# Two-layer decoder on one core: remainders of exponentials on two engines, a fourth staging buffer, scores by row groups

## The reference

```python
# layer 0
x = ln(einsum('bes,st->bet', x, Wr + Wc) + bias ...)        # mixing by decay matrices
s = einsum('bhqd,bhkd->bhqk', q, k) / 4                     # 16 heads of 16, 64 keys
attn = softmax(where(causal, s, min)); x = ln(x + (attn @ v) @ Wout.T)
e = argmax(x @ router_w); score = sigmoid(max(x @ router_w)) # 8 experts, one for each token
x = ln(x + expert_e(x * score) + shared(x))
# layer 1
x = ln(x + spectral_attention(x))      # DFT of normalised q, k; running sums over tokens
x = ln(x + latent_attention(x, ctx))   # 16 heads over 64 latent keys, softmax with causal mask
w = ternary(w_gate_up), ternary(w_proj)  # bf16, groups of 64: q = clip(round(w/mean|w|), -1, 1)
x = ln(x + swiglu(x, w) * rms)
```

## Time and profile before

| | us |
|---|---|
| median of 3 runs | 615.67 (613.36 to 617.16) |
| the profiled execution | 610.82 |
| its span, first to last instruction | 609.5 |
| PE busy | 553.6 |
| DVE busy | 472.8 |
| POOL busy | 389.4 |
| ACT busy | 369.8 |

### The profile page before, as it was taken

One profiled execution on the slowest core, in us unless ns is written; L12 is line 12 of the kernel. 1 busy time (PEld: TensorE's weight loads), 2 busy tenths in 40 slices (PEclk: granted clock), 3 DMA queues, 4 the chain that ended last, 5 costly groups with the idle time before them and its releaser, 6 DMA issues. The chain is left out here.

```text
span 609.5 us, 14270 instructions
## 1 busy us (share of the span) xinstructions
PE 553.6 (91%) x5331; PEld 436.6 (72%) x5331; DVE 472.8 (78%) x1266; ACT 369.8 (61%) x783; POOL 389.4 (64%) x467
## 2 busy tenths in 40 slices
PE   5789999889777999977899999999999999999995
PEld 3657887768654766643477888887877778889994
DVE  6896978796889675568899586689888898867656
ACT  5767588667643644545376567647665666655663
POOL 5839657678770440079999938775686644343896
PEclk9998999999899999999899999999999999999999
DMA  9132223104657443472010000022001200000001
GB/s 351 46 140 91 69 74 121 40 24 140 194 173 225 128 146 104 160 170 37 0 31 3 2 1 2 2 54 53 2 20 34 52 3 1 2 1 3 1 2 69
DMA packets 23696, 42.19 MB, mean 69 GB/s; under 512 B 3834, under 2 KB 18300, under 8 KB 23612
## 3 DMA queue, kind: packets, MB, share of 16 engines
q1 hardware_dynamic: 19900, 35.56, 17.9%
q0 software_dynamic: 3072, 4.20, 3.4%
q10 hardware_dynamic: 656, 1.52, 0.8%
HBM read 31.96 MB, written 10.35 MB: 69 GB/s over the span
## 5 line engine op out<-in xcount | busy, mean ns | idle before, releaser
L1761 DVE TENSOR_TENSOR first<-bank,first 128x512 f16<-128x512 f32 (+2 forms) x127 | 69.7, 564 | 14.0 <-ACT first L1627 5.9
L2216 POOL TENSOR_TENSOR first<-first 128x512 f16<-128x512 f32 x44 | 52.5, 1197 | 22.4 <-ACT first L1648 19.7
L1070 PE MATMUL bank<-wide,first 128*128 128x256 f16 (+4 forms) x199 | 54.3, 283 | 8.7 <-DVE first L1761 3.2
L1077 PE MATMUL bank<-c_first,first 128*128 128x128 f32 (+1 forms) x318 | 51.4, 280 | 3.8 <-ACT first L1580 1.8
L1071 PE MATMUL bank<-wide,first 128*128 128x256 f16 (+4 forms) x199 | 54.1, 282 | 0.0
L1072 PE MATMUL bank<-wide,first 128*128 128x256 f16 (+4 forms) x199 | 53.1, 281 | 0.0
L1077 PEld LDWEIGHTS bank<-c_first,first 128*128 128x128 f32 (+1 forms) x318 | 36.3, 140 | 12.2 <-ACT first L1580 4.7
L2194 POOL TENSOR_TENSOR first<-first,minus_half 128x2 f32<-128x2 f32 x30 | 22.3, 744 | 26.9 <-DVE first L1860 26.8
L2239 POOL DMA_INDIRECT wide<-made_rows,made_at x8 | 13.0, 1621 | 38.9 <-DMA made_rows<-first 35.0
L1761 DVE TENSOR_TENSOR wide<-bank,wide 128x512 f16<-128x512 f32 (+1 forms) x52 | 33.1, 651 | 4.8 <-ACT wide L1593 2.4
L2314 POOL TENSOR_TENSOR wide<-wide 128x512 f16<-128x512 f32 x16 | 18.6, 1160 | 23.4 <-ACT wide L1737 23.4
(11 more groups left out here) (465 smaller groups left out, 2108.4 us busy)
## 6 DMA issues: line engine op xcount, KB each, us to landing
wide<-in_fold SPq DMA_DIRECT2D x8, 992.0 KB, 5.2
wide<-in_expert SPq DMA_DIRECT2D x8, 768.0 KB, 4.7
wide<-in_ternary SPq DMA_DIRECT2D x8, 384.0 KB, 4.1
first<-sent_rows SPq DMA_DIRECT2D x20, 128.0 KB, 2.2
made_rows<-first SPq DMA_DIRECT2D x20, 128.0 KB, 1.9
x_mid<-first SPq DMA_DIRECT2D x7, 256.0 KB, 2.7
first<-in_x SPq DMA_DIRECT2D x4, 256.0 KB, 3.0
wide<-x_mid SPq DMA_DIRECT2D x4, 256.0 KB, 3.0
```

Of the source, the lines that this page charges most:

```text
L1070: mm(o, lhs[0], rhs[0], start=start, stop=False)
L1077: last = nc.tensor.transpose(view[0:m, c0:c0 + n], src, kc["identity" if dt == F32 else "identity_bf"][0:n, 0:n])
L1761: return V.tensor_tensor(lo, whole, hi, ALU.subtract)
L2216: G.tensor_tensor(B.pl[r], B.pf, B.ph[r], ALU.subtract).then_inc(says("ex_l"), 1)
```

## The change

Parts of it:

- Remainders of the first layer's exponentials: g = 0 and 2 stay on POOL (`ex_l`), g = 1 and 3 go to DVE (`ex_v`). The remainders of the gate and up weights of experts 4 and 6 go from POOL to DVE (`eg_lv`).
- A fourth staging buffer of 1560 words for three ternary blocks, laid over the shared expert's gate and up weights (`w_sgu`, not `w_sd`), so that its first load waits for all `rt` and `sh` of the first layer. Buffers 0 and 1 then have no ternary blocks. `t1` and `t2` move, and a lane of the second layer in `wide` ends earlier (`LANE1`).
- Maxima in four row groups: `mx` is now 128x(2x128) bf16, the 4 heads of group n at columns 32n to 32n + 3; `mt` is two 128x128 transposes in bf16, `mt_c` copies 128 rows, and in the first layer `minus_head` multiplies on the 32 rows of the group, with the bank as the inner loop. The causal matmuls come last. The second layer's `sc` keeps its matmuls on 128 rows.
- The count of a unit (`cnt`) is f32, `rk_seen` of unit 7 is gone, and `tb` sums `seen[7]` and the two `hot` tiles of unit 7 in three matmuls. `tb_cnt` has 3 waited steps for 5, `tb_tile` 5 for 9.
- Plan: new lengths, a part `begun` of 72 units ahead of the first loads, `keep_warm` from unit 2500 on, and another `RANKS`, so another order on every engine.

```diff
-    h = np.arange(NH)[:, None, None, None]
-    sel = -(h == 2 * np.arange(NP)[None, :, None, None] + np.arange(2)[None, None, :, None]).astype(np.float32)
-    c["minus_head"] = bf(np.concatenate([np.broadcast_to(sel, (NH, NP, 2, L)).reshape(NH, NP, P), np.zeros((P - NH, NP, P))]))
+    row = np.arange(P)[:, None, None, None]
+    pair, own = np.arange(NP)[None, :, None, None], np.arange(2)[None, None, :, None]
+    sel = -(row == P // ROWS * (pair // 2) + pair % 2 * 2 + own).astype(np.float32)
+    c["minus_head"] = bf(np.broadcast_to(sel, (P, NP, 2, L)).reshape(P, NP, P))
...
-EARLY_FOLDS, THIRD = 4, 5
+EARLY_FOLDS, THIRD, FOURTH = 4, 5, 3
...
-       + [("d", 0), ("b", 0)] + [("h", n) for n in range(EARLY_FOLDS, NPREP)] + [("f", n) for n in TERNARY[THIRD:]])
-TURNS = [[turn for n, turn in enumerate(ROW) if n % 2 == b] for b in range(2)] + [[("f", n) for n in TERNARY[:THIRD]]]
+       + [("d", 0), ("b", 0)] + [("h", n) for n in range(EARLY_FOLDS, NPREP)] + [("f", n) for n in TERNARY[THIRD + FOURTH:]])
+TURNS = [[turn for n, turn in enumerate(ROW) if n % 2 == b] for b in range(2)] + [[("f", n) for n in TERNARY[:THIRD]], [("f", n) for n in TERNARY[THIRD:THIRD + FOURTH]]]
...
+ON_VECTOR = (4, 6)
+
+
+def gate_up_rest(e):
+
+    return "eg_lv" if e in ON_VECTOR else "eg_lo"
+
+
+def shares_rest(u, g):
+
+    return "ex_v" if u < NB and g % 2 else "ex_l"
...
-    p.keep_warm(80, 0.7, 900)
+    p.keep_warm(80, 0.7, 2500)
...
+    LATE_STAGE = STAGES - 4 * (C * D + FSTAGE)
+    stages = [wide.tile([STAGE if n < 2 else FSTAGE]) for n in range(3)]
+    k.t1 = wide.tile([2, HEADS * DC], F32, 96)
+    k.t2 = wide.tile([HEADS, DC])
+    stages.append(wide.back(LATE_STAGE).tile([FSTAGE]))
     k.W = []
-    for n in range(3):
+    for n, stage in enumerate(stages):
...
-        B.mT = (a if n < LANES else shared).tile([S], BF16)
+        B.mx = (a if n < LANES else shared).tile([T, P], BF16)
...
-        B.cnt = a.tile([NE], F16)
+        B.cnt = a.tile([NE])
...
+        if b == 3 and n == 0:
+            sp.wait_ge(says("rt"), NB)
+            sp.wait_ge(says("sh"), 2 * NB)
...
-        flip(bank("mt", u), [(t * P, NH, lane(u).mx[:, t, :]) for t in range(T)]).then_inc(says("mt"), 1)
+        flip(bank("mt", u)[:, :].bitcast(BF16), [(t * P, P, lane(u).mx[:, t, :]) for t in range(T)], BF16).then_inc(says("mt"), 1)
...
-            for n, b in enumerate(banks):
-                mm(b[:, :].rearrange("p (n s) -> p n s", n=2)[:, :, 0:L], kc["identity_bf"], kc["causal_cols"], start=False, stop=False)
-                for m in range(C):
-                    last = mm(b[:, m * S:(m + 1) * S], kc["minus_head"][:, 2 * n + m, :], B.mT, start=False, stop=(m == C - 1))
+            for m in range(C):
+                for n, b in enumerate(banks):
+                    rows = slice(n * PAIR, (n + 1) * PAIR)
+                    mm(b[:, m * S:(m + 1) * S], kc["minus_head"][rows, 2 * n + m, :], B.mT[rows, :], start=False, stop=False)
+            for b in banks:
+                last = mm(b[:, :].rearrange("p (n s) -> p n s", n=2)[:, :, 0:L], kc["identity_bf"], kc["causal_cols"], start=False, stop=True)
...
-        pe.wait_ge(*done("ex_l", u, g))
+        pe.wait_ge(*done(shares_rest(u, g), u, g))
...
-        pe.wait_ge(*done("rk_seen", NB - 1))
-        mm(bank("tb", 0)[:, 0:NE], kc["all_ones"], k.seen[NB], start=True, stop=True).then_inc(says("tb"), 1)
+        pe.wait_ge(*done("rt_hot", NB - 1))
+        pe.wait_ge(*done("rk_seen", NB - 2))
+        counted = [k.seen[NB - 1]] + [lane(NB - 1).hot[:, t, :] for t in range(T)]
+        b = bank("tb", 0)
+        for n, some in enumerate(counted):
+            last = mm(b[:, 0:NE], kc["all_ones"], some, start=(n == 0), stop=(n == T))
+        last.then_inc(says("tb"), 1)
...
-        fn(lane(u).mT[0:NH, :], bank("mt", u)[0:NH, 0:S], ACT.Copy).then_inc(says("mt_c"), 1)
+        fn(lane(u).mT, bank("mt", u)[:, :].bitcast(BF16)[:, 0:S], ACT.Copy).then_inc(says("mt_c"), 1)
...
+    def eg_lv(u, e):
+        dve.wait_ge(*done("eg_hi", 0, e))
+        rest(k.w_egu[1][:, e, :], k.W[staged("e", e)[0]].eg.rearrange("p c n -> p (c n)"), k.w_egu[0][:, e, :]).then_inc(says("eg_lv"), 1)
...
+        m = lane(u).mx.rearrange("p t (q h) -> p t q h", q=ROWS)
+        return m[:, :, g, 0:4] if u < NB else m[:, g // 2, g % 2 * 2:g % 2 * 2 + 2, 0:4]
...
+    def ex_v(u, g):
+        B, r = lane(u), g % 2
+        dve.wait_ge(*done("ex_h", u, g))
+        dve.wait_ge(*done("ex_f", u, g))
+        if g > 1:
+            dve.wait_ge(*done("pv", u, g - 2))
+        rest(B.pl[r], B.pf, B.ph[r]).then_inc(says("ex_v"), 1)
...
-        dve.step(V.tensor_tensor(tab.cnt, bank("tb", 0)[:, 0:NE], kc["region_base"][:, 0, :], ALU.subtract))
-        dve.step(V.memset(tab.ones8, 1.0))
-        dve.step(V.tensor_scalar(tab.cnt_i, tab.cnt, float(P - 1), None, ALU.add))
+        base, given = kc["region_base"][:, 0, :], bank("tb", 0)[:, 0:NE]
+        V.memset(tab.ones8, 1.0)
+        dve.step(V.scalar_tensor_tensor(tab.cnt_i, given, float(P - 1), base, ALU.add, ALU.subtract))
+        V.tensor_tensor(tab.cnt, given, base, ALU.subtract)
...
+        before, no = slice(0, NE - 1), kc["tile_no"]
+        V.tensor_scalar(tab.past, tab.ends, no, None, ALU.is_le)
+        dve.step(V.scalar_tensor_tensor(tab.tmp, tab.ends, no, tab.nt, ALU.is_le, ALU.mult))
+        V.tensor_reduce(tab.ex, tab.past[:, before], AX.X, ALU.add)
+        V.tensor_scalar(tab.mine, tab.past[:, NE - 1:NE], float(P), float(-P), ALU.mult, ALU.add)
+        dve.step(V.tensor_reduce(tab.first, tab.tmp[:, before], AX.X, ALU.add))
+        V.tensor_copy(k.tile_exp, tab.ex)
+        V.scalar_tensor_tensor(tab.pick8, kc["expert_no"], tab.ex, tab.cnt, ALU.is_equal, ALU.mult)
+        dve.step(V.tensor_scalar(tab.begin1, tab.first, no, -1.0, ALU.subtract, ALU.add))
+        V.tensor_reduce(tab.cap, tab.pick8, AX.X, ALU.add)
+        dve.step(V.tensor_tensor(tab.at, tab.begin1, tab.mine, ALU.mult))
+        dve.step(V.tensor_tensor(tab.at2, tab.at, tab.cap, ALU.min))
+        V.scalar_tensor_tensor(k.tile_rows, tab.ex, float(REGION), tab.at2, ALU.mult, ALU.add).then_inc(says("tb_tile"), 1)
```

179 lines of the change are left out of this document (83 added, 96 removed).

## The result

| | before | after |
|---|---|---|
| median of 8 runs, us | 615.2 (613.4 to 617.2) | 611.2 (609.2 to 612.0) |
| ratio, 95% interval | | 0.9929 [0.9908, 0.9950] |
| profiled execution, us | 610.8 | 609.15 |
| span, us | 609.5 | 607.8 |

What follows compares the result with a forecast made beforehand. No one engine was taken to bound everything: PE the steady part and experts, POOL the filling, DVE fullest in the first layer. Terms -2 - 4 - 0 - 7 + 1 and -2 gave -14: 601.7 us from 615.67, range 588 to 616.

Steps and rivals of the forecast that it cites:

- the filling is not POOL's to give: Second layer's filling: gather, norm and prefix sums bound it, the fourth buffer gives only 2 us; 606.7 to 610.7, chance 0.20.
- Part 4: Second layer's filling, 280 to 320 us: a fourth staging buffer moves ternary blocks earlier; -7 us, between -2 and -14.
- So three are done near 235: Experts' stage: three ternary blocks chained through the new buffer from 180 on, 17 us for one block.
- the change doesn't move the blocks: Staging of ternary blocks: their loads would still be issued after 258; held hardly possible, no chance of its own given.
- POOL's 97%: Filling, 280 to 320 us: POOL busy 38.9 of 40 us, cited as evidence that POOL bounds this stage.
- would hold up an expert: SP's queue: a late ternary block delays the expert loads behind it; 0 to 3 us, taken as 0.
- Part 3: Table of expert rows: table and send start earlier, with fewer waited steps; -4 us, between -1 and -5.
- Part 2: First layer: remainders shared between POOL and DVE; the stage changes by -2 us, from -8 to +16.
- the 16 us of the rival: First layer: DVE, filled as before at 84%, bounds it and the stage takes 16 us more; 622 us, chance 0.14.
- Part 1: First layer's score matmuls on row groups: 6.7 us less PE work in all, 2 counted, between 0 and 6.
- Part 5: Every engine's queue: the new table of ranks may give or take 4 us, an estimate not priced from rows.
- The warm matmuls: First layer's start: keep_warm from 25 us instead of 9, PE perhaps at a lower clock; +1 us, 0 to 3.

Runs made afterwards that it cites:

- the second order: The changed kernel's parts in another searched order that prices late ternary blocks, the search gone on from the first such order; ratio 0.970 to the kernel before, 596.3 us.
- long_table_chain: The changed kernel with tb_cnt and tb_tile as before, 9 more dependent small operations, order unchanged; 608.2 us, ratio 0.989 to the kernel before.

## Why the prediction was wrong

The forecast of 601.7 missed by 9.5 us; the range of 588 to 616 held the time, since it was wide. The rival "the filling is not POOL's to give" (606.7 to 610.7) came nearest, but by luck: it took the blocks as moved, and they didn't move. By the prediction's own steps:

- **Part 4, the fourth buffer, -7: the step that failed.** "So three are done near 235" took for given that the order lets a free buffer be used at once. It doesn't: `fw`/`fw_c` of the block in the new buffer run at 255, and the three late blocks stay in the filling. The rival that said this, "the change doesn't move the blocks", I had put aside with "it hardly can be", since the wait on `sh` is met at 181; that load did come at 175, and the next one is what counts. That such blocks can be moved is shown by the orders with early blocks, where 6.8 us (10.2 in the second order) come back between gather and end. But only 3.1 and 6.1 of that lie behind the first DFT matmul, where the blocks can act, and the same work taken away in the changed kernel's own order gives 3.1 there. So the price of 7 was also too high, and POOL's 97% too simple a cause. A late block "would hold up an expert: 0 to 3 us, I take 0": no load of an expert, but that of the last folded head pair came 16.5 us later in the new order, and the stretch up to the first DFT matmul grew by 3.2 us. Whether the ternary loads in front of it on SP's queue or its place in the order did that isn't shown.
- **Part 3, the table, -4:** the table was 2.7 earlier, the load 0.6. The text named the rows' landing and took it for "as late as the table"; it is later, with four sends some 1.27 us apart. long_table_chain shows that the shorter chain is worth nothing while the rows come last. The f32 count left the stall as it was, 2.48 us.
- **Part 2, the turns, -2 for the stage:** DVE's cost was right. It has 142.4 us (forecast 145); the group of remainders with `ex_v` has a mean of 0.80 (I took 0.9) and a longest of 1.41 (bound 1.5). POOL has 102.9 where I had 91.6, as the new order does three ternary blocks in this stage, not two (7.3 us more). The turns' value, 4 us, was in the new order and none in the old one. The stage itself did not get 2 us shorter; its last `rt_hot` is 2.9 later. That is far from the 16 us of the rival, but whether DVE, at 91%, or something else held the stage isn't shown.
- **Part 1, -2:** PE's relief was right, the eight matmuls start within 0.1 us; in the time it can't be seen (0.991 without it, 0.993 with it).
- **Part 5, the order, 4 us either way:** here lay most of what could be had. Orders alone moved the old parts by 11 us and the new parts by 14 to 16 (0.993 to 0.970 and 0.967). Each set in its best order, the new parts are 7 to 10 us ahead of the old (0.967 and 0.970 against 0.982).
- **The warm matmuls, +1:** nothing that can be told.

Summed as the marks show: -0.6 up to the load, -0.3 more up to the gather, -0.8 behind it. The profiled executions differ by 1.7 us and the medians by 4.0; these two traces don't show the other 2.3. Both profiled executions were faster than the median of their kernel, by 4.4 and 2.0 us.

## What to carry to other kernels

Where every engine works off a fixed queue, a freed resource is worth only what the queues let it be: before pricing a buffer, look up where the parts that free it stand in the order, not when they could run. Price parts and order apart, by holding the order while a part is undone, and lay the order anew for each set of parts before a part is judged; here the same parts ran at 0.993, 0.990 and 0.967 of the kernel before. A search that minimises a plan is a proposal (ends planned within 1.5 us of one another came out up to 12 us apart), so measure several. And cut a stage at an event inside it before its time is put down to one cause: what was gained behind the first DFT matmul here was lost in front of it.
